# The last layer of a four-layer image network on one core: nine shifted taps from four helper arrays, and three stacked planes a chunk in their place

## The chip, the core and the metric

The kernel runs on one core of a Trainium2 chip. The metric is the device time of one execution in microseconds. The engines are TensorE (PE; PEld is its weight loading), VectorE (DVE), ScalarE (ACT), GpSimd (POOL) and SyncE (SP), which issues most transfers; 16 DMA engines carry them.

## What is computed

Input x is 8 images of 16 channels, 128 x 128, float32. Four layers follow each other, each of the form x = x + layer(groupnorm(x)). The change touches the last one alone: a 3 x 3 convolution with Kolmogorov-Arnold bases. Cut to what matters:

```python
patches = _extract_patches(x, 3, 1, 1)          # nine shifted copies, zero padded
bspl = _b_splines(patches, grid)                # eight cubic bases of each value
base_w = base_weight.sum(axis=2)
spl_w = (spline_weight * spline_scaler[..., None]).sum(axis=2)
out = jnp.einsum('bjhwn,ijn->bihw', jax.nn.silu(patches), base_w)
out = out + jnp.einsum('bjhwns,ijns->bihw', bspl, spl_w)
out = out + bias_weight[None, :, None, None]
x = x + out
```

## The kernel before

The layers run one after the other, each in blocks that end in a barrier. The first three (norm0 and layer0, layer1, layer2) stay as they are; layer2 leaves its result in the DRAM array out2, 16 channels by 8 images, each image as rows of 129 columns with padding. layer3 has two blocks.

The first block prepares. SP loads x2 (128 partitions: 8 images x 16 channels) and the eight images of out2 (L1385, each to 16 partitions). DVE adds them (L1420), copies the sum into a padded layout (L1421), takes the statistics (Norm.vector_part, L97 to L110) and normalises into Y (L1424). ACT applies silu to all of it (L1436). SP stores three arrays: x3q, the sum; g3q, the normalised input; s3q, its silu (L1388, L1391, L1394).

The second block starts with the weights (L1479) and with clearing on POOL (L1532). Its main loop walks the 134376 padded columns (all images in one line) in 66 passes of 2036 columns, plus one to finish. In a pass:

- SP loads gx, 16 channels of g3q broadcast to eight groups of 16 partitions, one group for each basis (L1487); si and si0, silu at the nine taps, each tap 16 channels from s3q (L1493, L1494); xr, the sum, in four quarters of 509 columns (L1496). It stores four quarters of the pass before the last into oq (L1501).
- ACT makes |x/h + place| (L1548), two relus (L1551, L1553) and their squares (L1556, L1558). DVE multiplies to cubes and adds them to the bases B (L1586, L1588, L1591).
- PE convolves: 8 matmuls for silu (L1608) and nine taps for the bases (L1617), each with 16 outputs padded to 32 columns of the array, one quarter in each of the four column groups.
- DVE adds bias and xr (L1579) and so gives SP leave (o_done) to load silu and xr of the pass after the next.

At the end SP copies oq to the output.

```python
for r, p in enumerate(AROUND):
    sp.dma_start(si[r * C:(r + 1) * C, k, :], s3q[:, bass.ds(g * SUP + (MARGIN + OFFS[p]), SUP)]).then_inc(si_in[k], 16)
```

The code of both blocks follows.

Of the kernel before, what the change touches and what calls it, by code (L numbers as in the profile page):

```python
# [4 lines left out]
F32 = mybir.dt.float32  # L5
# [6 lines left out]
P = 128  # L12
# [7 lines left out]
SUB = 509  # L20
# [10 lines left out]
MARGIN = 256  # L31
assert MARGIN >= max(OFFS)
# [1324 lines left out]
GRID_STEP = 2.0 / 5  # L1357

def layer3(nc, x2, out2, pair, l3w, x3q, g3q, s3q, oq, out):

    with ExitStack() as ctx:
        def sem(name):
            return ctx.enter_context(nc.semaphore(name))

        with ExitStack() as ctx1:
            def sb1(name, shape, dt=F32):
                return ctx1.enter_context(nc.sbuf_tensor(name, shape, dt))

            norm = Norm(nc, ctx1, "n3")
            X = sb1("l3_x", [P, HW])  # L1370
            Y = sb1("l3_y", [P, IMG])
            XP = sb1("l3_xp", [P, IMG])
            zero = sb1("l3_zero", [C, MARGIN + SUP])
            x_in, y_in = sem("l3_x_in"), sem("l3_y_in")
            chain = sem("l3_chain")
            x_ready, g_ready, s_ready, zeroed = sem("l3_x_ready"), sem("l3_g_ready"), sem("l3_s_ready"), sem("l3_zeroed")
            x_stored, stored = sem("l3_x_stored"), sem("l3_stored")

            with nc.Block() as block:
                @block.sync  # L1380
                def _(sp):
                    norm.sync_part(sp, pair)
                    sp.dma_start(X[:], x2).then_inc(x_in, 16)
                    for b in range(NB):
                        sp.dma_start(Y[b * C:(b + 1) * C, :], out2[:, SUP + b * IMG:SUP + (b + 1) * IMG]).then_inc(y_in, 16)  # L1385
                    sp.wait_ge(x_ready, 1)
                    for b in range(NB):
                        sp.dma_start(x3q[:, SUP + b * IMG:SUP + (b + 1) * IMG], XP[b * C:(b + 1) * C, :]).then_inc(x_stored, 16)  # L1388
                    sp.wait_ge(g_ready, 1)
                    for b in range(NB):  # L1390
                        sp.dma_start(g3q[:, b * IMG:(b + 1) * IMG], Y[b * C:(b + 1) * C, :]).then_inc(stored, 16)  # L1391
                    sp.wait_ge(s_ready, 1)
                    for b in range(NB):
                        sp.dma_start(s3q[:, MARGIN + SUP + b * IMG:MARGIN + SUP + (b + 1) * IMG], XP[b * C:(b + 1) * C, :]).then_inc(stored, 16)  # L1394
                    sp.wait_ge(zeroed, 1)

                    sp.dma_start(x3q[:, 0:SUP], zero[:, 0:SUP]).then_inc(stored, 16)
                    sp.dma_start(s3q[:, 0:MARGIN + SUP], zero[:]).then_inc(stored, 16)
                    sp.dma_start(s3q[:, MARGIN + SUP + LINE:], zero[:, 0:MARGIN]).then_inc(stored, 16)
                    sp.wait_ge(x_stored, NB * 16)  # L1400
                    sp.wait_ge(stored, (2 * NB + 3) * 16)

                @block.gpsimd
                def _(pool):
                    g = nc.gpsimd
                    g.memset(zero[:], 0.0).then_inc(zeroed, 1)
                    pool.wait_ge(x_ready, 1)

                    g.memset(Y[:, 0:PW], 0.0).then_inc(zeroed, 1)
                    g.memset(Y[:, PW:PW + H * PW].rearrange("p (h w) -> p h w", w=PW)[:, :, 0:1], 0.0).then_inc(zeroed, 1)  # L1410
                    g.memset(Y[:, PW + H * PW:], 0.0).then_inc(zeroed, 1)

                @block.vector
                def _(dve):
                    v = nc.vector
                    link = Chain(dve, chain)
                    link(v.memset(XP[:], 0.0))
                    dve.wait_ge(x_in, 16)
                    dve.wait_ge(y_in, NB * 16)
                    link(v.tensor_tensor(X[:], X[:], image_rows(Y), ALU.add))  # L1420
                    v.tensor_copy(image_rows(XP), X[:].rearrange("p (h w) -> p h w", w=W)).then_inc(x_ready, 1)  # L1421
                    norm.vector_part(dve, link, lambda k, n: X[:, k * n:(k + 1) * n], lambda e, k: None)
                    dve.wait_ge(zeroed, 4)
                    v.tensor_scalar(image_rows(Y), X[:].rearrange("p (h w) -> p h w", w=W), norm.rstd[:], norm.shift[:],  # L1424
                                    ALU.mult, ALU.add).then_inc(g_ready, 1)

                @block.tensor
                def _(pe):
                    norm.tensor_part(pe)

                @block.scalar
                def _(act):
                    norm.scalar_part(act)
                    act.wait_ge(g_ready, 1)
                    act.wait_ge(x_stored, NB * 16)
# [9 lines left out]
        wba = sb("l3_wba", [P, 2, 32])
        place = sb("l3_place", [P, 1])
        ends = sb("l3_ends", [P, 2])
        cbias = sb("l3_cbias", [P, 1])
        gx = sb("l3_gx", [P, 2, SUP])
        a = sb("l3_a", [P, SUP])  # L1450
        b = sb("l3_b", [P, SUP])
        a2 = sb("l3_a2", [P, SUP])
        b2 = sb("l3_b2", [P, SUP])
        B = sb("l3_bases", [P, BODY, SUP])
        si = sb("l3_si", [P, 2, SUP])
        si0 = sb("l3_si0", [P, 2, SUP])
        xr = sb("l3_xr", [P, 2, SUB])
# [12 lines left out]
        out_stored = sem("l3_out_stored")  # L1470
        stored = [sem("l3_o_stored0"), sem("l3_o_stored1")]
        STORE = NSUB * 16


        with nc.Block() as block:
            @block.sync
            def _(sp):
                for t, src in ((sw, l3w[0]), (scaler, l3w[1]), (bw, l3w[2]), (place, l3w[3]), (cbias, l3w[4])):
                    sp.dma_start(t[:], src).then_inc(w_in, 16)  # L1479
                sp.sem_inc(stored[0], 16)  # L1480
                sp.sem_inc(stored[1], 16)
                sp.wait_ge(cleared, 7)

                def load_bases_input(g, k, used):
                    sp.wait_ge(b_done, used)
                    src = g3q[:, bass.ds(g * SUP, SUP)].unsqueeze(0).broadcast_to([SPLINE, C, SUP])
                    sp.dma_start(gx[:, k, :], src).then_inc(gx_in[k], 16)  # L1487

                def load_silu(g, k):

                    sp.wait_ge(o_done, g + 1)
                    for r, p in enumerate(AROUND):
                        sp.dma_start(si[r * C:(r + 1) * C, k, :], s3q[:, bass.ds(g * SUP + (MARGIN + OFFS[p]), SUP)]).then_inc(si_in[k], 16)  # L1493
                    sp.dma_start(si0[0:C, k, :], s3q[:, bass.ds(g * SUP + MARGIN, SUP)]).then_inc(si_in[k], 16)  # L1494
                    for j in range(NSUB):
                        sp.dma_start(xr[32 * j:32 * j + C, k, :], x3q[:, bass.ds(g * SUP + j * SUB, SUB)]).then_inc(si_in[k], 16)  # L1496

                def store(g, k):
                    sp.wait_ge(o_done, g + 3)
                    for j in range(NSUB):  # L1500
                        sp.dma_start(oq[:, bass.ds(g * SUP + j * SUB, SUB)], O[32 * j:32 * j + C, k, :]).then_inc(stored[k], 16)  # L1501


                load_bases_input(0, 0, 1)
                for g in (0, 1):
                    load_bases_input(g + 1, (g + 1) % 2, g + 2)
                    load_silu(g, g)
# [253 lines left out]
```

## Time and profile before

| | us |
|---|---|
| median of 3 runs | 12673.22 |
| lowest and highest run | 12641.55, 12675.93 |
| span of the profiled execution | 12712.6 |
| PE busy | 9605.2 (76%) |
| DVE busy | 8869.0 (70%) |
| ACT busy | 7643.8 (60%) |
| POOL busy | 4796.5 (38%) |

The profiled execution's own time is given by its span alone, from its first instruction to its last; it is 39 us above the median. Busy time is a sum over all four layers, so it says little of the last one; views with a window do. A granted clock of 0.5 is 1.2 GHz, one of 1.0 is 2.4 GHz. DMA share is the mean busy share of the 16 DMA engines.

### The profile page before, as it was taken

How to read it: one execution, taken by the hardware profiler on the slowest of the kernel's cores; microseconds unless marked ns; L12 is line 12 of the kernel's file. 1: busy time of each engine (PE TensorE's matmuls, PEld its weight loads, DVE VectorE, ACT ScalarE, POOL GpSimd, SP SyncE). 2: the span in 40 equal slices, each digit the busy share in tenths (PEclk: the TensorE clock that was granted, in tenths of full speed). 3: DMA queues.
4: the chain of work that ended last, by engine and by line, in shares of the span. 5: the costliest groups of instructions: out<-in, count | busy, mean ns of one | idle time of the engine just before them, and what ended most of it. 6: DMA issues, size and time to landing. Idle time of an engine off the chain costs nothing. (4 is left out here: it accounts for less than half of the span.)

```text
span 12712.6 us, 210890 instructions
## 1 busy us (share of the span) xinstructions
PE 9605.2 (76%) x53759; PEld 4432.6 (35%) x53759; DVE 8869.0 (70%) x10861; ACT 7643.8 (60%) x11063; POOL 4796.5 (38%) x2382
## 2 busy tenths in 40 slices
PE   0888588868885888400999999999999999905565
PEld 0566366646663666100222222222222222202222
DVE  1877478748774777374888888888888888823343
ACT  0555255525552554232888888888888888815454
POOL 0333123212221322001666666666666666600000
PEclk9899689969996999755999999999999999957787
DMA  2000100010000000143111111111111111077787
GB/s 82 1 0 0 34 1 0 3 31 0 0 9 25 0 0 0 54 129 108 28 28 28 28 28 28 28 29 31 31 28 28 28 28 28 22 145 130 126 144 142
DMA packets 266253, 512.62 MB, mean 40 GB/s; under 512 B 46221, under 2 KB 205565, under 8 KB 260317
## 3 DMA queue, kind: packets, MB, share of 16 engines
q1 hardware_dynamic: 265314, 502.02, 18.1%
q8 instruction: 356, 5.83, 0.2%
q14 instruction: 583, 4.77, 0.1%
HBM read 368.49 MB, written 141.74 MB: 40 GB/s over the span
## 5 line engine op out<-in xcount | busy, mean ns | idle before, releaser
L1196 POOL TENSOR_TENSOR l_a<-l_a 128x1018 f32<-128x1018 f32 x1851 | 3453.2, 1883 | 1693.4 <-ACT l_a L1341 1678.5
L1311 DVE TENSOR_TENSOR l_r<-l_pps,l_a 128x509 f32<-128x509 f32 x4755 | 2988.7, 677 | 48.7 <-PE l_pps L1210 30.5
L1335 ACT ACTIVATE l_a<-l_qps 128x509 f32<-128x509 f32 x3705 | 2157.7, 597 | 822.0 <-PE l_qps L1210 568.8
L1341 ACT ACTIVATE l_a<-l_a 128x1018 f32<-128x1018 f32 x2380 | 2504.3, 1052 | 39.8 <-issue 39.8
L1210 PE MATMUL l_qps<-l_mv,l_wst 123*128 123x509 bf16 x4235 | 1645.0, 389 | 172.3 <-ACT l_a L1335 54.2
L1210 PE MATMUL l_pps<-l_mv,l_wst 123*128 123x509 bf16 x4228 | 1626.2, 385 | 63.7 <-DVE l_r L1311 60.9
L654 POOL TENSOR_TENSOR a_pr<-a_pr 128x768 f32<-128x768 f32 x384 | 898.4, 2339 | 1641.6 <-DVE a_pr L569 1626.6
L683 ACT ACTIVATE a_g<-a_fps 128x512 f32<-128x512 f32 x1152 | 680.6, 597 | 1023.7 <-PE a_fps L436 1022.3
L436 PE MATMUL a_fps<-a_hbt,a_wfc 96*128 96x512 f32 x2304 | 1238.1, 674 | 70.4 <-ACT a_g L683 70.4
L407 PEld LDWEIGHTS a_cps<-a_wfp,a_g 128*128 128x128 f32 x9216 | 1139.1, 200 | 207.7 <-issue 158.1
L1299 DVE TENSOR_SCALAR l_a<-l_qps 128x509 int32<-128x509 int32 x1058 | 724.7, 685 | 688.7 <-PE l_qps L1210 678.2
L454 POOL TENSOR_TENSOR a_pr<-a_qkv 128x768 f32<-128x768 f32 x128 | 386.5, 3037 | 2088.8 <-ACT a_qkv L696 2088.8
L407 PE MATMUL a_cps<-a_wfp,a_g 128*128 128x48 f32 (+1 forms) x9216 | 1126.5, 281 | 40.9 <-DVE a_x2c L582 40.9
L1266 PE MATMUL l_sps<-l_r,l_sums 128*32 128x509 f32 x8448 | 1132.3, 608 | 8.6 <-DVE l_r L1311 8.2
L1210 PEld LDWEIGHTS l_qps<-l_mv,l_wst 123*128 123x128 bf16 x4235 | 407.8, 96 | 2080.6 <-ACT l_a L1335 1414.9
L1305 DVE TENSOR_TENSOR l_a<-l_a 128x1018 f32<-128x1018 f32 x529 | 800.0, 1512 | 89.6 <-ACT l_a L1341 88.6
L569 DVE TENSOR_TENSOR a_pr<-a_qkv,a_at 128x768 f32<-128x768 f32 x576 | 810.1, 1459 | 2.2
L1608 PE MATMUL l_ops<-l_si,l_wba 128*32 128x509 f32 x1072 | 217.6, 954 | 612.9 <-DMA l_xr<-x3q 572.2
L436 PEld LDWEIGHTS a_fps<-a_hbt,a_wfc 96*128 96x128 f32 x2304 | 428.1, 211 | 580.6 <-ACT a_g L683 341.4
L1210 PEld LDWEIGHTS l_pps<-l_mv,l_wst 123*128 123x128 bf16 x4228 | 413.5, 98 | 506.8 <-DVE l_r L1311 365.5
L1225 PE MATMUL l_ops<-l_s,l_pick 128*32 128x509 f32 (+5 forms) x5360 | 571.4, 512 | 0.0
L1617 PE MATMUL l_ops<-l_bases,l_wsp 128*32 128x509 f32 (+8 forms) x5896 | 566.8, 538 | 0.0
(169 smaller groups left out, 11983.2 us busy)
## 6 DMA issues: line engine op xcount, KB each, us to landing
l_mv<-pw SPq DMA_DIRECT2D x1608, 79.5 KB
l_si<-s3q SPq DMA_DIRECT2D x603, 127.2 KB, 8.1
l_gx<-g3q SPq DMA_DIRECT2D x66, 1018.0 KB
pw<-pw_hi SPq DMA_DIRECT2D x165, 127.2 KB
pw<-pw_mid SPq DMA_DIRECT2D x165, 127.2 KB
pw<-pw_lo SPq DMA_DIRECT2D x165, 127.2 KB
a_tb<-g SPq DMA_DIRECT2D x16, 1031.9 KB
out<-l_o SPq DMA_DIRECT2D x268, 31.8 KB, 2.8
```

What stands on the lines that cost most here:

```text
L407: last = t_.matmul(cps[:, c % 2, j * F2 + lo:j * F2 + hi], G[:, g % 2, m, j * P:(j + 1) * P], wfp[:, m, lo:hi], start=m == 1, stop=m == 2, ...
L436: t_.matmul(fps[:, n % 2, :], wfc[:, m * P:(m + 1) * P], hBT[:, g * 4:(g + 1) * 4, :].rearrange("f w h -> f (w h)"), start=True, stop=True ...
L569: v.tensor_tensor(out, val, a, ALU.mult).then_inc(val_v, 1)
L654: g_.tensor_tensor(y, y, PR[:, 3 * d + e, :], ALU.add).then_inc(val_p, 1)
L1196: g.tensor_tensor(a, a, a, ALU.mult).then_inc(sq_p, 2)
L1210: return t.matmul(out, wst[:, k, n * P:(n + 1) * P], x[:, n // NPP, cols], start=True, stop=True)
L1266: last = t.matmul(sps[32 * pp:32 * pp + 32, 0:SUB], sums[:, 0, :], R[:, (m - NPP + 1 + pp) % R_RING, :], start=n == NPP - 1, stop=n == NPA ...
L1299: v.tensor_scalar(A[:, s % A_RING, :].bitcast(I32), qps[:, s % Q_BANKS, 0:SUB].bitcast(I32), 0x7FFFFFFF, None, ALU.bitwise_and).then_inc(a ...
L1305: v.tensor_tensor(a, a, a, ALU.mult).then_inc(sq_v, 2)
L1311: v.tensor_tensor(R[:, m % R_RING, :], pps[:, m % P_BANKS, 0:SUB], A[:, m % A_RING, :], ALU.mult).then_inc(mul_done, 1)
L1335: s_.activation(A[:, s % A_RING, :], qps[:, s % Q_BANKS, 0:SUB], ACT.Abs).then_inc(abs_a, 1)
L1341: s_.activation(a, a, ACT.Abs_reciprocal_sqrt, bias=1.0).then_inc(root_done, 2)
```

## The change

Only layer3 and its weights' layout change. Chunks are now four image rows of 130 columns (CHN = 520), 33 chunks with the padding. A chunk has two units, e = 0 and 1, each of four images side by side (2080 columns).

- Preparation: x2 and out2 come in eight pieces of 16 rows, and DVE adds and takes statistics piece by piece. The sum stays in SBUF (X). Only the normalised input is stored, into g3, chunk by chunk. The weights are loaded and summed in this block too.
- Bases: ACT makes the distance (L1543) and two squares; the two slopes now come from DVE (L1591, L1593), POOL subtracts the cubes (L1625, one operation a unit).
- Spline part: for each dx one matmul with 48 of 64 output columns, the three tap rows dy stacked on the output partitions; both units side by side in the array. ACT copies the planes to SBUF, and PE adds the three planes with shifted rows by 0/1 matrices (pick).
- Silu part: computed on ACT once a chunk (L1550) from gs, which holds the normalised input of two image rows of taps, dy = 0 in the lower 64 partitions and dy = 1 in the upper; gs is loaded by six transfers a chunk, and has one buffer.
- The result is added into X and stored from there into the output.

The diff, cut to the order on the queues and the operations of the new loop:

```diff
@@ layer3, first block @@
-                    for b in range(NB):
-                        sp.dma_start(Y[b * C:(b + 1) * C, :], out2[:, SUP + b * IMG:SUP + (b + 1) * IMG]).then_inc(y_in, 16)
...
+                    for k in range(PIECES):
+                        n = HW // PIECES
+                        sp.dma_start(X[:, k * n:(k + 1) * n], x2[:, k * n:(k + 1) * n]).then_inc(x_in[k], 16)
+                        if k >= 3:
+                            sp.wait_ge(added, k - 2)
+                        at = SUP + PW + k * ROWS * PW
+                        rows = out2[:, SUP:].rearrange("c (b n) -> b c n", b=NB)[:, :, at - SUP:at - SUP + ROWS * PW]
+                        sp.dma_start(Y[:, k % 3, :], rows).then_inc(x_in[k], 16)
...
+                        for j in range(QUAD):
+                            to = g3[lo:hi, :, :, j, :].rearrange("k e c n -> (e c) k n")
+                            src = G[32 * j:32 * j + 32, lo * CROWS:hi * CROWS, :].rearrange("p (k r) w -> p k (r w)", r=CROWS)
+                            sp.dma_start(to, src).then_inc(g_stored, 16)
@@ layer3, second block, SP @@
-                def load_silu(g, k):
-
-                    sp.wait_ge(o_done, g + 1)
-                    for r, p in enumerate(AROUND):
-                        sp.dma_start(si[r * C:(r + 1) * C, k, :], s3q[:, bass.ds(g * SUP + (MARGIN + OFFS[p]), SUP)]).then_inc(si_in[k], 16)
...
+                for n in range(NUNIT):
+                    k, e = divmod(n, PARITY)
+                    if n >= GX:
+                        sp.wait_ge(bases, n - GX + 1)
+                    src = g3[k, e].rearrange("c j n -> c (j n)").unsqueeze(0).broadcast_to([SPLINE, C, UNIT])
+                    sp.dma_start(gx[:, n % GX, :], src).then_inc(gx_in[n % GX], 16)
+                    if e == 0:
+                        if k:
+                            sp.wait_ge(silu_done, k)
+                        for h in range(HALF):
+                            rows = g3[k].rearrange("e c j n -> j (e c) n")[2 * h:2 * h + 2]
+                            sp.dma_start(gs[0:64, h, :], rows).then_inc(gs_in, 16)
+                            sp.dma_start(gs[64:P, h, 0:CHN - QW], rows[:, :, QW:]).then_inc(gs_in, 16)
+                            if k + 1 < NCK:
+                                below = g3[k + 1].rearrange("e c j n -> j (e c) n")[2 * h:2 * h + 2, :, 0:QW]
+                                sp.dma_start(gs[64:P, h, CHN - QW:], below).then_inc(gs_in, 16)
+                    elif k >= 4:
+                        store(k - 4)
@@ ACT @@
+                distance(0)
+                for n in range(NUNIT):
+                    k, e = divmod(n, PARITY)
+                    if n + 1 < NUNIT:
+                        distance(n + 1)
...
+                    s_.activation(a2[:, n % 2, :], na[:, n % 2, :], ACT.Square).then_inc(a2_done, 1)
...
+                    s_.activation(b2[:], gx[:, n % GX, :], ACT.Square, scale=2.0).then_inc(b2_done, 1)
+                    if n >= 3:
+                        for j in (0, 1) if e else (2, 3):
+                            keep((n - 3) // PARITY, j)
+                    if e == 1:
+                        silu(k)
@@ ACT, silu(k) @@
+                    pieces = (k + 1) * 6 if k + 1 < NCK else k * 6 + 4
+                    act.wait_ge(gs_in, pieces * 16)
...
+                    s_.activation(S[:, k % PSLOTS, :, :], gs[:], ACT.Silu).then_inc(silu_done, 1)
@@ DVE @@
+                    v.tensor_scalar(na[:, n % 2, :], x, 2.0, 0.0, ALU.subtract, ALU.min).then_inc(na_done, 1)
...
+                    v.tensor_scalar(x, x, 1.0, 0.0, ALU.subtract, ALU.min).then_inc(nb_done, 1)
...
+                    v.tensor_tensor(a2[:, n % 2, :], a2[:, n % 2, :], na[:, n % 2, :], ALU.mult).then_inc(a3_done, 1)
...
+                    v.tensor_tensor(gx[:, n % GX, :], b2[:], gx[:, n % GX, :], ALU.mult).then_inc(b3_done, 1)
@@ POOL @@
+                    g_.tensor_tensor(B[:, e, :, at:at + CHN], gx[:, n % GX, :].rearrange("p (j n) -> p j n", j=QUAD),
+                                     a2[:, n % 2, :].rearrange("p (j n) -> p j n", j=QUAD), ALU.subtract).then_inc(bases, 1)
@@ PE @@
+                        for dx in range(3):
+                            for e in range(PARITY):
+                                x = B[:, e, j, at:at + CHN].rearrange("p (r w) -> p r w", w=QW)[:, :, dx:dx + W]
+                                last = t.matmul(pps[64 * e:64 * e + 64, m % PBANKS, :].rearrange("p (r w) -> p r w", w=W), wsp[:, dx, :],
+                                                x, start=dx == 0, stop=dx == 2, skip_group_check=True)
...
+                    for dy in range(3):
+                        for to, n, row in pieces(k, dy):
+                            for j in range(QUAD):
+                                last = t.matmul(rows_out[32 * j:32 * j + 32, to:to + n, :], pick[:, dy, :],
+                                                planes[:, j, row:row + n, :], start=False, stop=dy == 2, skip_group_check=True)
...
+                multiply(0)
+                for k in range(NOUT):
+                    multiply(k + 1)
+                    gather(k)
```

Where the order moves, on the engines that wait. SP's queue in the main loop before, as the program lists it (the instruction, output and input tile, the size, what it waits for; "x7" is a repeat). This is a pass after the loop's unrolled part:

```order
L1487 DMA l_gx<-g3q 128x1x2036 [waits l3_b_done]
L1493 DMA l_si<-s3q 16x2036 [waits l3_o_done]
L1493 DMA l_si<-s3q 16x2036 x7
L1494 DMA l_si<-s3q 16x2036
L1496 DMA l_xr<-x3q 16x509 x4
L1501 DMA oq<-l_o 16x509 [waits l3_o_done]
L1501 DMA oq<-l_o 16x509 x3
```

And SP's queue in the changed kernel, one chunk of the steady loop, from gs(k) to the first load for gs(k+1):

```order
L1525 DMA l_gs<-g 64x1x520 [waits l3_silu_done]
L1526 DMA l_gs<-g 64x1x390
L1529 DMA l_gs<-g 64x1x130
L1525 DMA l_gs<-g 64x1x520
L1526 DMA l_gs<-g 64x1x390
L1529 DMA l_gs<-g 64x1x130
L1519 DMA l_gx<-g 128x1x2080 [waits l3_bases_ready]
L1512 DMA out_x<-l_x 128x512 [waits l3_o_done]
L1519 DMA l_gx<-g 128x1x2080 [waits l3_bases_ready]
L1525 DMA l_gs<-g 64x1x520 [waits l3_silu_done]
```

The silu input has moved behind a wait for ACT's silu of the chunk before, and the input of the chunk's second unit stands behind it.

ACT's queue in the changed kernel, from one silu to the next (l_gx<-l_gx is the distance, l_planes the copies of planes, l_s<-l_gs the silu):

```order
L1550 ACTIVATE l_s<-l_gs 128x1040 [waits l3_o_made,l3_gs_in]
L1543 ACTIVATE l_gx<-l_gx,l_place 128x2080 [waits l3_gx_in1]
L1568 ACTIVATE l_a<-l_na 128x2080 [waits l3_na_done,l3_bases_ready]
L1572 ACTIVATE l_b<-l_gx 128x2080 [waits l3_b3_done,l3_nb_done]
L1557 ACTIVATE l_planes<-l_pps 128x512 [waits l3_o_made,l3_plane_made] x2
L1543 ACTIVATE l_gx<-l_gx,l_place 128x2080 [waits l3_gx_in2]
L1568 ACTIVATE l_a<-l_na 128x2080 [waits l3_na_done,l3_bases_ready]
L1572 ACTIVATE l_b<-l_gx 128x2080 [waits l3_b3_done,l3_nb_done]
L1557 ACTIVATE l_planes<-l_pps 128x512 [waits l3_o_made,l3_plane_made] x2
L1550 ACTIVATE l_s<-l_gs 128x1040 [waits l3_o_made,l3_gs_in]
```

Silu and the copies of planes are new on ACT, the two relus have left it, and the first instruction behind a silu is a distance.

## Rows read from the trace of the kernel before

**Rows 1.** The page: DMA share in 40 slices, and the chain that ended last.
```profile
DMA  2000100010000000143111111111111111077787
...
DMA l_xr<-x3q 4%; PE l_ops L1617 2%; PE l_ops L1608 1%; SPq L1493 1%; SPq L1496 0%; DVE l_o L1579 0%; SPq L1494 0%; POOL l_bases L1532 0%; DVE l_bases L1591 0%; DVE l_a L1586 0%; DVE l_b L1588 0%; SPq L1501 0%; SPq L1487 0%; POOL l_si L1532 0%; DVEq L1578 0%
```

**Rows 2.** Windows: length, busy PE, PEld, DVE, ACT, POOL; clock, DMA share, GB/s.
```profile
11150.00:11415.00 265.00, 1.14 (x4) 1.00 (x4) 70.08 (x46) 17.03 (x4) 2.60 (x4) 0.50 0.81 163
11415.00:11430.00 15.00, 0.00 (x0) 0.00 (x0) 0.00 (x0) 0.00 (x0) 14.50 (x3) 0.50 0.27 98
11430.00:12678.00 1248.00, 768.54 (x6968) 305.95 (x6968) 498.49 (x269) 625.02 (x330) 0.54 (x5) 0.78 0.77 132
12678.00:12712.60 34.60, 0.00 (x0) 0.00 (x0) 0.68 (x1) 0.00 (x0) 0.00 (x0) 0.55 0.86 246
```

**Rows 3.** Groups by line from 11430 us on: busy, mean ns | idle before.
```profile
L1608 PE MATMUL l_ops<-l_si,l_wba 128*32 128x509 f32 x1072 | 217.6, 954 | 612.9 <-DMA l_xr<-x3q 572.2 <-DVE l_bases L1591 39.8 <-DVE l_o L1579 1.0
L1586 DVE TENSOR_TENSOR l_a<-l_a 128x2036 f32<-128x2036 f32 x66 | 150.3, 2278 | 284.2 <-ACT l_a L1556 284.2
L1548 ACT ACTIVATE l_gx<-l_gx,l_place 128x2036 f32<-128x2036 f32 x66 | 131.5, 1992 | 629.5 <-DMA l_gx<-g3q 629.4
L1556 ACT ACTIVATE l_a<-l_a 128x2036 f32<-128x2036 f32 x66 | 124.4, 1885 | 3.4 <-DVE l_bases L1591 3.4
L1579 DVE SCALAR_TENSOR_TENSOR l_o<-l_ops,l_cbias,l_xr 128x509 f32<-128x509 f32 x67 | 50.2, 749 | 455.9 <-PE l_ops L1617 455.9
```

**Rows 4.** Chain of waits in the main loop: start, length, what.
```profile
11678.22 0.76 DVE l_o L1579
11685.51 21.19 DMA l_xr<-x3q
11706.83 3.62 PE l_ops L1608 x16
11710.45 8.68 PE l_ops L1617 x50
11719.28 0.76 DVE l_o L1579
```

**Rows 5.** Windows, one transfer each: 127 partitions, x2, l_y, stores of g3q, l_gx.
```profile
140.00:160.00 20.00, 0.00 (x0) 0.00 (x0) 0.00 (x0) 0.00 (x0) 0.00 (x0) 1.00 0.07 20
11155.00:11167.00 12.00, 0.00 (x0) 0.00 (x0) 12.00 (x1) 0.00 (x0) 0.00 (x0) 0.50 0.98 426
11175.00:11235.00 60.00, 0.00 (x0) 0.00 (x0) 0.00 (x0) 0.00 (x0) 0.00 (x0) 0.50 1.00 114
11310.00:11340.00 30.00, 0.00 (x0) 0.00 (x0) 0.00 (x0) 0.00 (x0) 0.00 (x0) 0.50 0.96 251
11447.00:11456.00 9.00, 0.00 (x0) 0.00 (x0) 0.00 (x0) 7.49 (x4) 0.00 (x0) 0.50 0.52 119
```
**Rows 6.** Timeline of the preparation: start, length, what.
```profile
11150.97 4.11 SPq L1385 DMA_DIRECT2D l_y<-out  x8
11247.91 17.23 DVE L1420 TENSOR_TENSOR l_x<-l_x,l_y 128x16384 f32<-128x16384 f32 x1 [80.20 <-DMA l_y<-out]
11292.90 1.02 DVE L99 BATCH_NORM_AGGREGATE n_own<-n_stats 128x2 f32<-128x192 f32 x1
...
11297.14 8.81 DVE L1424 TENSOR_SCALAR l_y<-l_x,n_rstd,n_shift 128x16384 f32<-128x16384 f32 x1
...
11415.50 0.36 SPq L1479 DMA_DIRECT2D l_sw<-in_w_spline  x1
11430.57 1.44 SPq L1487 DMA_DIRECT2D l_gx<-g3q  x2
```

**Rows 7.** The page's groups in layer 2: POOL's product, ACT's PSUM copy and root.
```profile
L1196 POOL TENSOR_TENSOR l_a<-l_a 128x1018 f32<-128x1018 f32 x1851 | 3453.2, 1883 | 1693.4 <-ACT l_a L1341 1678.5
L1335 ACT ACTIVATE l_a<-l_qps 128x509 f32<-128x509 f32 x3705 | 2157.7, 597 | 822.0 <-PE l_qps L1210 568.8
L1341 ACT ACTIVATE l_a<-l_a 128x1018 f32<-128x1018 f32 x2380 | 2504.3, 1052 | 39.8 <-issue 39.8
```

More of the change, by code:

```diff
@@ L1357, with layer3, sb @@
 GRID_STEP = 2.0 / 5
-def layer3(nc, x2, out2, pair, l3w, x3q, g3q, s3q, oq, out):
+QW = W + 2
+CROWS = 4
+CHN = CROWS * QW
+NCK = (H + 2 + CROWS - 1) // CROWS
+NOUT = H // CROWS
+PARITY, QUAD = 2, NB // 2
+UNIT = QUAD * CHN
+GX, BSLOTS, PSLOTS, PBANKS = 3, 2, 3, 6
+HALF = 2
+assert QUAD * 32 == P and NCK == NOUT + 1
+def layer3(nc, x2, out2, pair, l3w, g3, out):
     with ExitStack() as ctx:
+        def sb(name, shape, dt=F32):
+            return ctx.enter_context(nc.sbuf_tensor(name, shape, dt))
         def sem(name):
             return ctx.enter_context(nc.semaphore(name))
+        X = sb("l3_x", [P, HW])
+        wsp = sb("l3_wsp", [P, 3, 64])
+        wba = sb("l3_wba", [P, 2, 3, QUAD, C])
+        pick = sb("l3_pick", [P, 3, 32])
+        place = sb("l3_place", [P, 1])
+        cbias = sb("l3_cbias", [P, 1])
+        mask = sb("l3_mask", [P, QUAD])
         with ExitStack() as ctx1:
@@ L1367, in sb1 @@
                 return ctx1.enter_context(nc.sbuf_tensor(name, shape, dt))
+            PIECES = 8
+            ROWS = H // PIECES
             norm = Norm(nc, ctx1, "n3")
[L1370 to L1377, printed above, removed]
+            Y = sb1("l3_y", [P, 3, ROWS * PW])
+            G = sb1("l3_g", [P, NCK * CROWS, QW])
+            sw = sb1("l3_sw", [P, 9, 9, C])
+            scaler = sb1("l3_scaler", [P, 9, 9, C])
+            bw = sb1("l3_bw", [P, 9, 9, C])
+            x_in = [sem(f"l3_x_in{k}") for k in range(PIECES)]
+            w_in = sem("l3_w_in")
+            added, chain = sem("l3_added"), sem("l3_chain")
+            zeroed, g_ready, g_stored = sem("l3_zeroed"), sem("l3_g_ready"), sem("l3_g_stored")
             with nc.Block() as block:
@@ L1389, in _ @@
[L1389 to L1397, printed above, removed]
@@ L1416, in _ @@
                     link = Chain(dve, chain)
[L1417 to L1423, printed above, removed]
@@ L1445, in layer3 @@
[L1445 to L1457, printed above, removed]
@@ L1477, in _ @@
             def _(sp):
[L1478 to L1487, printed above, removed]
@@ L1498, in store @@
[L1498 to L1507, printed above, removed]
-                with sp.Fori(1, NSUP // 2 - 1) as it:
-                    for k in range(2):
-                        g = it * 2 + k
-                        load_bases_input(g + 1, 1 - k, g + 2)
-                        load_silu(g, k)
-                        store(g - 2, k)
```

335 lines of the change are left out of this document (178 added, 157 removed).

## The prediction

> **What bounds the kernel now.** Read the page first, then windows by stage, then the chain of waits inside the last stage. The page's DMA row shows the last fifth of the span at seven or eight tenths while every compute engine is at five or less, and its chain of waits ends in loads of l_xr [rows 1]. The windows give the stages [rows 2]: 265 us of preparation of the last layer (x2 plus layer 2's output, norm, stores of three helper arrays), 15 us of clearing, 1248 us of main loop, 35 us of a final copy. Everything ahead of 11150 us is untouched by the change, so the question is 1562 us against what replaces them.
>
> The main loop makes 67 passes in 1248 us, 18.6 us each. In a pass PE needs about 12 us, the three DVE operations of 2036 columns 6.8, the five ACT operations 9.7 [rows 3]. None is full. The chain repeats one piece: last matmul, DVE's finish, thirteen loads issued by SP in about 6.5 us, 21 us until the last lands, 12 us of matmul; two passes are in flight, so 41 us of it carry two [rows 4]. DMA is the bound, at 132 GB/s with a share of 0.77 [rows 2]. Why so slow? [Rows 5] hold five kinds of transfer. Whole 128-partition rows go at 426 GB/s with all engines busy. Loads that write 16 neighbouring partitions (l_y) keep all engines busy and yet move 114. The broadcast l_gx, whose outermost dimension is 8 copies, keeps a share of 0.52 busy and moves 119. Layer 0's load of 127 partitions keeps 0.07 busy, 20 GB/s. I read two things from this: the share follows the outermost dimension (8 of 16 engines, 1 of 16), and a busy engine moves 27 GB/s in the first kind, only 14 in l_gx (119 over 8.3 engines), because engines that walk blocks of partitions get in each other's way.
>
> **The change, part by part.** The span of this profile, 12712.6 us, stands 39 us (0.3%) above the median of the runs, 12673.2; I sum against the span and carry the difference over. 0.3% is also about what a measurement of this kernel can tell from no change.
>
> *Preparation.* Now: loads 11151 to 11248, add 17.2, copy, statistics, norm, normalise 8.8, store g, silu, store s, until 11415.5; first l_gx issued at 11430.6 after the clearing [rows 6]. After: x2 and out2 come in eight pieces, add and statistics follow each piece, one array is stored. The out2 pieces have an outermost dimension of 8, like l_gx: 8.45 MB at 119 GB/s is 71 us on eight engines; x2 adds 8.4 MB at 426, 20 us; the weights, 2 MB, 5 us. So 96 us, as long as now. Then the last piece, 17.2/8 for the add and four statistics at 0.6 to 0.9 (the copy and 32 of them fill the 28 us from the add's end to 11292.9), 5 us, the norm's tail 4.2 (11292.9 to 11297.1), the first normalised piece 8.8/8 = 1.1, and 8.65 MB of stores at the 251 GB/s of today's stores, 35 us, with 5 us for landing and the barrier. Start of the new loop: 11150.5 + 146 = 11297, against 11415.5 for the old one. That saves about 119 us; the l3_x copy, silu pass and two arrays of stores are gone. Bounds on the stores, which now have rows of 2080 bytes: 20 us (426 GB/s) to 65 (132 GB/s), so 90 to 134 saved.
>
> *Main loop.* 33 chunks of two units of 2080 columns. Costs per chunk, scaled from [rows 3] and [rows 7]: ACT 2 x (1.99 + 2 x 1.89) x 2080/2036 = 11.8, four copies of planes at 0.6 = 2.4, one silu of 1040 columns 1.1 (1.05 for 1018), waits between them 0.7: 16 us. DVE 4 products of 2.33, 4 slopes of about 1.2 (0.54 ns a column as in the 8.8 us of normalising), finish 0.75: 15 us. POOL 2 subtractions at 1.85 ns a column: 7.7. PE: a round of four 32-column matmuls takes 1.81 us at granted clock 0.5 (16 records, two rounds, in 3.62 [rows 4]) and 0.9 when warm (nine rounds in 8.7, the first of them still slow); 12 rounds of two 64-column matmuls for the planes, 6 for silu, 3 for the shifted adds, 21 x 0.9 = 19 us. Transfers: two l_gx of 1.06 MB at 119 GB/s, 17.8, plus l_gs. If all of this overlapped, a chunk would take some 20 us. It does not overlap, because of the order on SP and ACT.
>
> ACT runs distance(n+1) before the squares of unit n, and silu(k) at the end of unit 2k+1. SP issues l_gx(2k), then **waits for silu(k-1)**, then issues six l_gs loads, and only then l_gx(2k+1). But distance(2k+1) is the very next thing that ACT does after silu(k-1). l_gs has one buffer, so this wait can't pass early. Every chunk thus pays, one after the other: silu(k-1) done, six l_gs, l_gx(2k+1), then ACT's 16 us up to silu(k). DVE, POOL and PE are behind ACT in that circle and cover nothing of it.
>
> The l_gs price: 532 KB in six loads whose source has an outermost dimension of 2. The row of 127 partitions and that of l_gx say that such a load runs on 2 of the 16 engines. No row shows two engines. Bounds: 27 GB/s each, 9.8 us; or 11 each (132 GB/s over the 12 busy engines of the main loop), 24 us. I take 14 each, the rate of l_gx, since here too each engine walks a block of partitions: 19 us. Behind it on the same two engines come their sixteen rows of l_gx(2k+1), 133 KB each, 4.9 to 9.5 us; I take 7. First issue 0.65, landing about 2. Gap: 0.65 + 19 + 7 + 2 = 29 us (17 to 36).
> The Trainium skill, page DMA: Bandwidth & Descriptors, section "Why a DMA increments its semaphore by 16 and not by 1", says that a DMA uses the largest number up to 16 that divides the outermost sizes of both sides: 2 here, and it speaks against this change. The page SBUF — State Buffer, section "Door 1: The DMA port swizzle", says that partitions 32 apart share a port of 27.2 GB/s; the two engines start 32 apart, and by it l_gs would take 19.6 us as an estimate.
>
> PE adds one more wait. After the second pair of planes of a chunk is copied, PE does 3 rounds of shifted adds and 6 rounds of the next planes before ACT's next copies can both run. PE has idled some 25 us by then, so two rounds go at clock 0.5, as in each pass now: 3.6 + 7 x 0.9 = 10 us, against 6 of ACT work and the copy between: 3 us exposed (0 to 8).
>
> Chunk: 29 + 16 + 3 = 48 us. Loop: 33 x 48 + 30 for the last planes, sum, finish and store (in the first chunk the gap is paid as filling) = 1614. The final copy (35 us) is gone, since finish writes straight into X and out.
> Before, from 11415.5 to the end: 1297. So +317 in the loop, -119 in the preparation: **+198**, span 12911, median **12870 us**, 1.6% slower. The loop's transfers fall from 165 MB to 96 MB, and still the time rises: the bytes saved ran in parallel, the new wait doesn't.
>
> **Rivals.**
> A, faster: l_gs is cheap. Either two engines at full rate (9.8 us, then 5 for l_gx: gap 18, chunk 37) or all 16 (532 KB at 119 GB/s 4.5 us, l_gx 8.7: gap 16, chunk 35). Loop 1185 to 1251, total 12441 to 12507; up to 12600 with small rows a little slower than 27. It wins when the chunk is under 40.5 us, that is when l_gs takes under 12. For it: a single engine alone moves 17 to 20 in the 127-partition row, even in rows of 520 bytes. Against: l_gx's 14. The change would then pay mostly by its preparation.
> B, slower yet: 64-column matmuls of the two halves don't run side by side. No row has that width; only 32-column ones, four at once, are shown. Then the planes need 12 rounds instead of 6 before ACT's copies, and the exposed wait grows from 3 to about 9: chunk 54, total 13070.
> C, in between: l_gs at 20 GB/s an engine, 13 us, gap 22, chunk 41: 12640, no measurable change.
>
> **Numbers.** Forecast 0.57 (12750 to 13000), B 0.10, C 0.07, A 0.26. Point 12870. The range must keep most of A and reach to B: 12480 to 13100. Faster by over 0.3% 0.26, within 0.07, slower 0.67.
>
> **What would show it.** In the loop ACT should idle 25 to 30 us ahead of one Abs in two, released by the l_gx load, for some 900 us in all, with a DMA share near 0.13 in the second half of that idle time (eight engines and then only two at work), and about 48 us between silus. PE's granted clock stays well under 1. The new loop starts near 11297. If the gap before the odd Abs is under 20 us, A holds. If ACT waits longest for PE's planes, B. Should ACT not idle at that Abs at all, my reading of the order is wrong, and the time would be near 11950.

## The result, and the profile after

The changed kernel takes 12784.51 us (median of 4 runs, 12773.45 to 12785.26) against 12674.58 for the kernel before beside it: a ratio of 1.0087, with a 95% interval of 1.0064 to 1.0109. It is slower by 110 us, where the forecast was 198 slower. Its page, with the same parts as [rows 1]:

```profile
span 12783.1 us, 200441 instructions
...
PEclk9899689969997998755999999999999999957777
DMA  2000100010000000043111111111111111142222
...
DMA l_gx<-g 5%; DVE l_a L1606 1%; POOL l_bases L1625 1%; DVE l_na L1591 1%; ACT l_gx L1543 0%; DVE l_gx L1609 0%; PE l_pps L1652 0%; DVE l_gx L1593 0%; PE l_ops L1681 0%; ACT l_b L1572 0%; ACT l_a L1568 0%; SPq L1529 0%; SPq L1526 0%; SPq L
```

The last slices have fallen from seven and eight tenths to two: the engines that carry transfers are now mostly idle, and yet the chain ends in a transfer, l_gx. The waits of the last 1480 us of the changed kernel (engine, line, released by: us in total, times, longest):

```profile
POOL l_bases L1625 <- DVE l_gx L1609: 1219.9, 64, 195.1
ACT l_gx L1543 <- DMA l_gx<-g: 893.7, 34, 50.1
DVE l_na L1591 <- ACT l_gx L1543: 857.4, 34, 41.5
...
ACT l_planes L1557 <- PE l_pps L1652: 140.2, 66, 10.0
```

ACT waits 34 times for l_gx, 894 us in all; 34 is one in two of 66 loads and the start, which has the longest, 50.1. All else hangs on it: DVE waits for ACT and POOL for DVE. Start and end of the parts, from the timeline of the changed kernel, which answers to [rows 6]:

```profile
11262.53 10.14 DVE L1475 TENSOR_SCALAR l_g<-l_x,n_rstd,n_shift 128x2048 f32<-128x2048 f32 x8
11263.90 32.30 SPq L1429 DMA_DIRECT2D g<-l_g  x32
11300.25 0.60 SPq L1519 DMA_DIRECT2D l_gx<-g  x1
```

And the line of silu (L1550): its count, duration, first and last start.

```profile
L1550 ACT ACTIVATE l_s<-l_gs x33: 1060/1062/1077, 11349.4 to 12749.0; 128x1040 f32<-128x1040 f32 x33
```

The loop begins at 11300.25, and 32 chunks lie between the first silu and the last: (12749.0 - 11349.4)/32 = **43.7 us a chunk**. One of them, from silu to silu:

```profile
11960.40 1.06 ACT L1550 ACTIVATE l_s<-l_gs 128x1040 f32<-128x1040 f32 x1
...
11961.49 0.51 SPq L1525 DMA_DIRECT2D l_gs<-g  x1
...
11963.92 4.62 POOL L1625 TENSOR_TENSOR l_bases<-l_gx,l_a 128x2080 f32<-128x2080 f32 x1 [5.72 <-DVE l_gx L1609]
...
11964.62 2.82 SPq L1529 DMA_DIRECT2D l_gs<-g  x1
...
11967.49 1.63 SPq L1519 DMA_DIRECT2D l_gx<-g  x1
...
11986.60 2.03 ACT L1543 ACTIVATE l_gx<-l_gx,l_place 128x2080 f32<-128x2080 f32 x1 [25.14 <-DMA l_gx<-g]
...
11993.30 4.99 PE L1681 MATMUL l_ops<-l_planes,l_pick 128*32 128x512 f32 x24 [23.13 <-ACT l_planes L1557]
...
11995.78 5.51 POOL L1625 TENSOR_TENSOR l_bases<-l_gx,l_a 128x2080 f32<-128x2080 f32 x1 [27.24 <-DVE l_gx L1609]
11996.84 5.56 DVE L1593 TENSOR_SCALAR l_gx<-l_gx 128x2080 f32<-128x2080 f32 x1
...
11998.22 10.09 PE L1652 MATMUL l_pps<-l_bases,l_wsp 128*64 128x512 f32 x46
...
12003.64 0.60 ACT L1557 ACTIVATE l_planes<-l_pps 128x512 f32<-128x512 f32 x1 [1.98 <-PE l_pps L1652]
12004.13 1.06 ACT L1550 ACTIVATE l_s<-l_gs 128x1040 f32<-128x1040 f32 x1
```

The order is the forecast one: silu, six l_gs issues, l_gx behind them, and ACT idle for 25.14 us until it lands; the other 18.6 us are ACT's circle. The transfers in that gap and just behind it, in windows of 2 us (us, busy time of PE, PEld, DVE, ACT, POOL, granted clock, DMA share, GB/s):

```profile
11964.00:11966.00 2.00, 2.00 (x12) 0.70 (x10) 0.44 (x1) 0.00 (x0) 2.00 (x1) 1.00 0.13 48
11966.00:11968.00 2.00, 2.00 (x14) 0.85 (x12) 0.00 (x0) 0.00 (x0) 2.00 (x1) 1.00 0.13 48
11970.00:11972.00 2.00, 0.17 (x2) 0.00 (x0) 0.00 (x0) 0.00 (x0) 0.00 (x0) 1.00 0.56 183
...
11980.00:11982.00 2.00, 0.00 (x0) 0.00 (x0) 0.00 (x0) 0.00 (x0) 0.00 (x0) 0.50 0.55 155
...
11984.00:11986.00 2.00, 0.00 (x0) 0.00 (x0) 0.00 (x0) 0.00 (x0) 0.00 (x0) 0.50 0.46 133
...
11988.00:11990.00 2.00, 0.00 (x0) 0.00 (x0) 1.31 (x2) 2.00 (x2) 0.00 (x0) 0.50 0.14 54
```

A share of 0.13 is two engines of sixteen, and alone they move 48 GB/s, 24 each. The first bytes of l_gs move about 2 us after the end of silu, and the two engines have the time up to about 11969 to themselves, 5.5 us: some 260 KB of the 532. The l_gx, issued at 11967.49, shows in the share only after that. From then on its eight engines are at work, and so are the store of the output and the next l_gx, l_gx(2k+2), issued 1.7 and 2.8 us behind it: the share stays near a half until the wait ends. The two engines then still owe some 270 KB of l_gs and their 266 KB of l_gx, 268 KB each, and have moved them when the l_gx has landed, 17.6 us later: 15 GB/s each, worked out from the bytes. When that l_gx has landed, two engines are left with the next one, and the last window shows them at 54 GB/s with a share of 0.14, some 24 each again.

**Where the time went.** The first three layers, which the change leaves alone, do not take the same time in every execution: in the profiled executions of the table below the last layer began between 11083.8 and 11159.9. The kernel before, timed beside each group of them, had medians from 12660 to 12702, so a difference of a few tens of us between medians says little. So kernels are compared below by their medians, and by the last layer of the profile alone, from its first load of x2 or of out2 to the end. Before, that was 12712.6 - 11150.5 = 1562.1 us; after, 12783.1 - 11149.2 = 1633.9: +72.

### The profile page after: what moved, and what is told of

Read it like the earlier page. It is cut to its first block and busy times, and to the rows that moved or that the text cites. A ratio compares the mean times of both kernels' runs of the same rounds, so it can differ in the third digit from the quotient of the medians.

```text
span 12783.1 us, 200441 instructions
## 1 busy us (share of the span) xinstructions
PE 9480.8 (74%) x50455; PEld 4341.6 (34%) x50455; DVE 8979.9 (70%) x10918; ACT 7480.8 (59%) x11095; POOL 5115.3 (40%) x2443
## 5 line engine op out<-in xcount | busy, mean ns | idle before, releaser
L1625 POOL TENSOR_TENSOR l_bases<-l_gx,l_a 128x2080 f32<-128x2080 f32 x66 | 334.8, 5073 | 1269.3 <-DVE l_gx L1609 1219.9
L1681 PE MATMUL l_ops<-l_planes,l_pick 128*32 128x512 f32 (+3 forms) x928 | 147.6, 802 | 727.3 <-ACT l_planes L1557 727.3
L1591 DVE TENSOR_SCALAR l_na<-l_gx 128x2080 f32<-128x2080 f32 x66 | 81.9, 1241 | 857.4 <-ACT l_gx L1543 857.4
L1543 ACT ACTIVATE l_gx<-l_gx,l_place 128x2080 f32<-128x2080 f32 x66 | 133.7, 2025 | 893.7 <-DMA l_gx<-g 893.7
```

## The experiments

Two theories stood against each other. **Theory:** the loop waits for one chain, silu(k-1), six l_gs on two engines, l_gx(2k+1); both the order and the two engines make it. **Rival:** the bound is elsewhere (l_gx on its eight engines alone, or POOL, DVE and PE behind the loads), and the l_gs loads only hide it. Each edit was made to the changed kernel if nothing else is said.

| kernel | median us | ratio to before (95%) | last layer us | chunk us |
|---|---|---|---|---|
| changed | 12784.51 | 1.0087 (1.0064 to 1.0109) | 1633.9 | 43.7 |
| e1, l_gx first | 12420.06 | 0.9779 (0.9736 to 0.9823) | 1259.3 | 32.0 |
| e2, l_gs on 16 engines | 12545.9 | 0.9879 (0.9834 to 0.9923) | 1380.2 | 36.1 |
| e3, l_gx on 16 engines | 12655.91 | 0.9964 (0.9931 to 0.9997) | 1520.0 | 40.2 |
| e4, all three | 12116.99 | 0.9542 (0.9506 to 0.9579) | 955.9 | 23.3 |
| e5b, no l_gs | 12185.01 | 0.9604 (0.9518 to 0.9690) | 1058.6 | 26.0 |
| e9, subtraction on DVE | 12775.01 | 1.0069 (1.0040 to 1.0098) | 1646.1 | 44.0 |
| e8, e4 and e9 | 12012.99 | 0.9483 (0.9447 to 0.9519) | 888.3 | 20.9 |
| e7, kernel before, l_gx on 16 | 12391.16 | 0.9778 (0.9733 to 0.9824) | 1239.4 | |

A chunk is worked out as above, from the first and last start of silu.

**e1: both l_gx of a chunk ahead of the wait.** One place in SP's program:

```diff
-for n in range(NUNIT): wait for bases; load l_gx(n)
-    if e == 0: wait for silu(k-1); load l_gs(k)
+for n in range(NUNIT):
+    if e == 0: load_gx(n); load_gx(n + 1)
+               wait for silu(k-1); load l_gs(k)
```

> SP issues both l_gx loads of a chunk ahead of its wait for silu(k-1); nothing else changes, l_gs keeps its six loads on few engines. Order theory (the odd unit's load waits behind silu(k-1) and six l_gs loads): ACT's idle time of 25 us before every second Abs goes; what is left is what two DMA engines carry in a chunk, l_gs 14 us and two l_gx 9 us each, about 32 us against 44, so 12400 to 12450 us. Rival (the load of l_gs on two engines is the bound whatever the order): the time of l_gs and l_gx on the two engines already fills the chunk, so within 0.3% of 12784. Rival (PE's planes hold ACT): also no change beyond 2 us a chunk.

12420.06 us, as the theory says. Nothing but the order changed, and 364 us went. What is left of the gap, in its timeline:

```profile
11800.01 2.03 ACT L1548 ACTIVATE l_gx<-l_gx,l_place 128x2080 f32<-128x2080 f32 x1 [16.98 <-DMA l_gx<-g]
...
11806.55 1.06 ACT L1555 ACTIVATE l_s<-l_gs 128x1040 f32<-128x1040 f32 x1
11807.51 2.02 ACT L1548 ACTIVATE l_gx<-l_gx,l_place 128x2080 f32<-128x2080 f32 x1
...
11815.15 10.86 SPq L1519 DMA_DIRECT2D l_gx<-g  x2
...
11832.42 2.03 ACT L1548 ACTIVATE l_gx<-l_gx,l_place 128x2080 f32<-128x2080 f32 x1 [18.26 <-DMA l_gx<-g]
```

The Abs right after silu no longer waits. The wait has moved to the even unit and is shorter, 17 to 18 us: the next l_gx follows the l_gs in the queue of the same engines.

**e2: l_gs in twelve loads of 32 partitions.** The source row j of the four, taken alone, has an outermost dimension of 32:

```diff
-rows = g3[k].rearrange("e c j n -> j (e c) n")[2 * h:2 * h + 2]
-sp.dma_start(gs[0:64, h, :], rows)
+rows = g3[k].rearrange("e c j n -> j (e c) n")[j]
+sp.dma_start(gs[lo:lo + 32, h, :], rows)
```

> Order on SP as in the changed kernel; each l_gs load is cut into two of 32 partitions, with the 32 as the outermost dimension, 12 loads a chunk instead of 6. Two-engine theory: l_gs now runs on all 16 engines and takes 4 us instead of 14, but SP needs 6 us to issue twelve; the gap falls from 25 to 16 to 18 us, chunk 35 to 37, 12480 to 12550 us. Rival (l_gs is limited by its row size, not by its engines): gap unchanged or 3 us longer by the issues, 12780 to 12880.

12545.9 us, inside what the theory gave for it. The same bytes, in twice as many loads. Its DMA issues between 11360 and 12700 us (count, KB each, median us to landing):

```profile
l_gs<-g SPq DMA_DIRECT2D x124, 65.0 KB, 2.0
l_gs<-g SPq DMA_DIRECT2D x124, 48.8 KB, 1.9
l_gs<-g SPq DMA_DIRECT2D x120, 16.2 KB, 1.7
```

Each lands about 2 us after its issue, so SP's issuing, twelve in 5.5 us, is what they cost now:

```profile
11812.44 1.06 ACT L1552 ACTIVATE l_s<-l_gs 128x1040 f32<-128x1040 f32 x1
...
11813.53 0.31 SPq L1527 DMA_DIRECT2D l_gs<-g  x1
...
11818.99 0.60 SPq L1519 DMA_DIRECT2D l_gx<-g  x1
...
11830.93 2.03 ACT L1545 ACTIVATE l_gx<-l_gx,l_place 128x2080 f32<-128x2080 f32 x1 [17.43 <-DMA l_gx<-g]
```

**e3: l_gx on sixteen engines.** The basis partitions are ordered (channel, copy) instead of (copy, channel), in the load and in the weights, so that the outermost dimension is 16:

```diff
-src = g3[k, e].rearrange("c j n -> c (j n)").unsqueeze(0).broadcast_to([SPLINE, C, UNIT])
+src = g3[k, e].rearrange("c j n -> c (j n)").unsqueeze(1).broadcast_to([C, SPLINE, UNIT])
```

> The bases' partition order is turned from (copy, channel) to (channel, copy), so the broadcast source of l_gx has an outermost dimension of 16 instead of 8; weights are laid out to match. Engine-count theory: l_gx runs on 16 engines, at least 1.5 times as fast (9 us to 4 to 6); the gap falls from 25 to about 20 us because l_gx comes last in it, chunk 39, 12600 to 12660 us. Rival (l_gx is limited where it lands, not by its engines): same 9 us, within 0.3% of 12784.

12655.91 us: 129 us less, near the top of the expected range. The two engines of l_gs now owe half as much l_gx, but the six l_gs stand ahead as before, and the chunk is still 40.2 us. Of the three edits this one alone gives least.

**e4: all three.**

> The three edits together. Theory: no transfer is waited for any more; the chunk is bounded by DVE (about 19 us a chunk with its stalls beside POOL) and PE (19 us), chunk 21 to 25, 12010 to 12150 us, faster than both kernels by 4 to 5%. Rival (a second circle over PE's planes and ACT's copies takes over, 4 us of wait a chunk are seen already): chunk 27 to 30, 12220 to 12320.

12116.99 us, inside the range. The three save 668 us together, where one by one they save 364, 239 and 129, 732 in sum: they cut the same gap, so they do not quite add. One part of the expectation failed: l_gx is still waited for, now ahead of every Abs, by 3.6 to 4.8 us in the chunks around 11725, and 333.5 us in all:

```profile
ACT l_gx L1550 <- DMA l_gx<-g: 333.5, 66, 45.6
```

**e5: the l_gs loads left out** after the first chunk, so that silu is taken of chunk 0's rows 33 times and the output is not the layer's.

```diff
-if k:
-    sp.wait_ge(silu_done, k)
-load l_gs(k)
+if not k:
+    load l_gs(0)
```

> The six silu loads of every chunk but the first are left out: silu is taken of chunk 0's rows 33 times, all else stays. Theory (the gap of 25 us ahead of one Abs in two is made by these loads, which run on two of the sixteen DMA engines and stand ahead of the second l_gx): a chunk of 43.7 us falls to the circle of the three l_gx slots, some 24 to 26 us, as in the kernel with all three edits (23.3), a little above it since l_gx still runs on eight engines; 32 x 18 to 19.5 us off 12784: 12160 to 12210 us. Rival (the loads only hide a bound of the computation, POOL's subtraction and the DVE operations beside it being slower than before): the chunk stays above 30 us, 12350 us or more.

One execution took 12227.9 us; the profiled one ran with PE's granted clock at 0.27 and took 33169 us, so nothing is read from it. It was run again:

> The kernel of e5_no_gs once more: the profiled execution there took 33169 us with a TensorE clock of 0.27 in the records, and its only other execution 12228 us. As there: the silu loads of every chunk but the first are left out. Theory (the two-engine loads ahead of the second l_gx make the gap): a chunk of 24 to 26 us, 12160 to 12230 us, and no gap of 25 us ahead of an Abs in the trace. Rival (a bound of the computation behind them): chunks above 30 us, 12350 us or more.

12185.01 us and 26.0 us a chunk, the theory's numbers. So l_gs cost 17.7 of 43.7 us, with all that went with it: its 532 KB a chunk, its issues and SP's wait for silu, which the edit takes out together. The computation was no bound above 26 us. Its timeline has waits of five or six us for l_gx, ahead of every Abs, and none of 25:

```profile
11807.37 2.03 ACT L1542 ACTIVATE l_gx<-l_gx,l_place 128x2080 f32<-128x2080 f32 x1 [5.33 <-DMA l_gx<-g]
...
11820.38 2.03 ACT L1542 ACTIVATE l_gx<-l_gx,l_place 128x2080 f32<-128x2080 f32 x1 [6.36 <-DMA l_gx<-g]
```

e4 beats it by 68 us (103 by the last layer alone) while it loads everything: l_gs is hidden there, and l_gx arrives sooner.

**e6: a second buffer for the silu input** and nothing else, so that its loads need not wait for the silu of the chunk before. It was expected to take 12370 to 12530 us, or to change nothing. It gave no time: with the second buffer the planes no longer fit into SBUF (24576 bytes a partition wanted, 23872 left). What the wait alone costs, with l_gs kept ahead of l_gx, is therefore not measured.

**e7: the kernel before, with the l_gx order of e3.** If [rows 5] were read rightly, the kernel before was itself waiting for eight engines.

> The kernel before, with the basis partitions ordered (channel, copy) so that the outermost dimension of the l_gx load is 16 instead of 8. Theory (its last loop waits for eight of the sixteen engines, which the trace shows full while the mean share is 0.76): l_gx spreads over all sixteen, the loop shortens from 1297 us towards 0.76/0.98 x 1297 = 1006 us, where the engines are evenly full; 12684 - 150 to 290 = 12395 to 12535 us. Rival (the sixteen engines share one bound on what 128 partitions take in, so that the spread changes nothing): within 30 us of 12684.

12391.16 us, 2.2% faster than the kernel before and 393 us faster than the changed one. Windows of 1280 us of the loop before, and of 500 us in e7 (columns as above):

```profile
11420.00:12700.00 1280.00, 768.54 (x6968) 305.95 (x6968) 499.18 (x269) 625.02 (x330) 10.54 (x5) 0.78 0.76 133
```

```profile
11500.00:12000.00 500.00, 391.12 (x3847) 161.44 (x3839) 272.89 (x147) 350.71 (x185) 0.00 (x0) 0.90 0.98 182
```

All sixteen engines are now full, at 182 GB/s instead of 133. The rival, that 128 partitions take in no more than before, has fallen. It also gives both designs with their l_gx on sixteen engines: e4 against e7, 12117 against 12391. That is not the worth of the stacked planes alone. By the last layer e4 is 283.5 us shorter, and 131 of them lie ahead of the first l_gx, in preparation and clearing (150 us against 281).

**e9: the subtraction on DVE instead of POOL.** The profile's chain through the chunk above runs over POOL's subtraction, begun at 11963.92, to l_gx, issued at 11967.49. POOL takes 5.07 us on average and one slope on DVE takes 5.56 beside it, where the same operation alone takes 1.24.

```diff
-pool: wait for a3, b3, plane_made; g_.tensor_tensor(B[...], gx[...], a2[...], ALU.subtract).then_inc(bases, 1)
+dve:  wait for a3, b3, plane_made; v.tensor_tensor(B[...], gx[...], a2[...], ALU.subtract).then_inc(bases, 1)
```

> The changed kernel with one edit, the subtraction on DVE instead of POOL. Theory (the gap is a gap of transfers, and POOL's subtraction stands on the chain only between it and the next load into the same slot: 5.07 us on POOL beside 3.3 us slopes, against 2.3 and 1.24): 2 to 4 us of 43.7 in a chunk, 12784 - 65 to 130 = 12650 to 12720 us. Rival (the subtraction is hidden behind the gap, as the wait of the loads is for the silu of the chunk before, which follows the Abs and not the subtraction): within 35 us of 12784.

The rival is right. 12775.01 us is the changed kernel's time within the intervals, and a chunk stays at 44.0 us. The timeline shows why:

```profile
11961.72 2.03 ACT L1543 ACTIVATE l_gx<-l_gx,l_place 128x2080 f32<-128x2080 f32 x1 [25.49 <-DMA l_gx<-g]
...
11970.86 2.33 DVE L1615 TENSOR_TENSOR l_bases<-l_gx,l_a 128x2080 f32<-128x2080 f32 x1
...
11980.19 2.32 DVE L1615 TENSOR_TENSOR l_bases<-l_gx,l_a 128x2080 f32<-128x2080 f32 x1
...
11984.49 1.34 SPq L1529 DMA_DIRECT2D l_gs<-g  x1
11985.87 1.65 SPq L1519 DMA_DIRECT2D l_gx<-g  x1
```

The load of the odd unit, l_gx(2k+1), waits for the bases of unit 2k-2, whose slot it takes. Here that subtraction is done at 11973.19, and l_gx still goes out at 11985.87, behind the last l_gs issue. In the changed kernel it is this one:

```profile
11952.67 5.53 POOL L1625 TENSOR_TENSOR l_bases<-l_gx,l_a 128x2080 f32<-128x2080 f32 x1 [28.52 <-DVE l_gx L1609]
```

It ended at 11958.20, 9.3 us before the l_gx. The subtraction that the chain names runs from 11963.92 for 4.62 us, to 11968.54, and was still running when l_gx was issued; the chain cuts it off at that moment. It cannot have released this load, only l_gx(2k+2), at 11970.29.

**e8: the same edit on e4**, where the gap is gone.

> The kernel with all three edits (12117), and the subtraction that makes the bases moved from POOL to DVE. Theory (a chunk there, 23.3 us, is two thirds of the circle of one l_gx slot, some 35 us from the issue of its load to the end of the subtraction; POOL's subtraction takes 4.6 us where DVE takes 2.3, and while it runs the first DVE slope takes 3.4 us on average instead of 1.24): the circle falls by some 4 us, and DVE is busy 2 x (2 x 1.24 + 3 x 2.32) + 0.75 = 19.6 us in a chunk, which then bounds it: 20.5 to 22 us a chunk, 12117 - 32 x (1.3 to 2.8) = 12030 to 12075 us. Rival (the two engines do not slow each other, the long slope is only a wait that the profile counts as work): DVE gets 4.6 us more in a chunk, and the time stays or rises, 12100 to 12180 us.

12012.99 us, 5.2% below the kernel before and the fastest here. It lies 17 us below the expected range in the median, while the chunk, 20.9 us, lies inside it. The first slope (L1598) in e4 and then in e8, shortest, median and longest in ns:

```profile
L1598 DVE TENSOR_SCALAR l_na<-l_gx x66: 1244/3434/3839, 11307.1 to 12053.7; 128x2080 f32<-128x2080 f32 x66
```

```profile
L1598 DVE TENSOR_SCALAR l_na<-l_gx x66: 1230/1243/1246, 11293.8 to 11967.8; 128x2080 f32<-128x2080 f32 x66
```

Same operation, same data, 3.43 us beside a POOL subtraction and 1.24 without: the two engines do hold each other up, and here it counts. By the last layer alone the edit saves 67.6 us. The medians differ by 104; in the two profiles e8's last layer begins 21.8 us earlier, after layers that the edit leaves alone, and the rest of the difference is not explained by any row.

## Why the prediction came out as it did

**What bounds the kernel: right.** The engines at work follow the outermost dimension (e2, e3, e7), and l_gx on eight engines was the bound before (e7). The second reading of [rows 5], 14 GB/s for an engine of l_gx, held beside other engines. Its reason, that engines which walk blocks of partitions get in each other's way, was not tested, but two such engines alone move 24 each.

**Preparation: right.** The loop was to begin at 11297 and begins at 11300.25: the first piece is normalised at 11262.5, where the sum gave 11256, and the issues of the stores of g took 32.3 us of the 35 allowed. Some 115 us of 119 were saved.

**The order on SP and ACT: right.** This was the step on which the sign hung. The gap stands ahead of one Abs in two (893.7 us in all, the start with them, 900 forecast), released by l_gx, and reordering alone (e1) takes the chunk from 43.7 to 32.0.

**The l_gs price: too high, and the term that missed.** The gap was put at 29 us and is 25.1. "I take 14 each, the rate of l_gx" nearly holds for a load beside l_gx: the two engines move 15 GB/s each in the last 17.6 us. It does not hold for the 5.5 us before, in which l_gs is alone and they move 24 each, near the upper bound of 27. The two rates belong to one chain, and the forecast used the low one for all of l_gs. Worked out from these rates, l_gs takes 5.5 + 9 = 14.5 us where the sum had 19, and the two engines' share of l_gx 8.7 where it had 7; the first 2 us, in which no byte moves, complete the 25.1. By the issues, the gap is 6.0 us from the end of silu to the issue of l_gx and 19.1 to its landing. The Trainium skill's page DMA: Bandwidth & Descriptors, section "Why a DMA increments its semaphore by 16 and not by 1", gives 2 engines here, and the share of 0.13 agrees. The forecast's estimate from its page SBUF — State Buffer, section "Door 1: The DMA port swizzle", that two engines starting 32 partitions apart have the 27.2 GB/s of one port between them, does not hold: they moved 48. The section says which partitions share a port; that both engines are at the same port at the same moment was the forecast's own step, and no row shows where each of them stood.

**The sign in the DMA share: missed.** A share near 0.13 was to stand in the second half of the idle time, with eight engines and then only two at work. It stands at the beginning, before l_gx; the second half has 0.46 to 0.55. The forecast had left out that SP issues the next chunk's first l_gx only 2.8 us behind the one waited for: the engines that are done with that one go on with the next, beside the two that are late. This is where the 15 GB/s were measured, and no run has the two without it.

**ACT's circle and PE's wait: right in sum.** 16 + 3 = 19 forecast, 18.6 measured. ACT's exposed wait for PE is 140.2 us over the loop, 4.2 a chunk against 3. The 46 matmul records of 64 columns in the chunk above take 10.09 us. A matmul is two records, a round of the forecast two matmuls, and so a round takes 10.09 x 48/46/12 = 0.88 us, 0.9 forecast. Were the two of a pair run one after the other at 0.9 each, a round would take twice that; rival B has fallen.

**DVE and POOL: sized too low, and it cost nothing.** Slopes of "about 1.2" take up to 5.6 beside POOL, and POOL's subtraction 5.07 instead of 3.85. e9 shows that the gap hid it, e8 that it costs 2.4 us a chunk once the gap is gone.

**The sum.** 32 x (48 - 43.74) = 136 us are more than the miss in the last layer, 126: 198 forecast and 72 measured. The first chunk's filling (49.1 us against 48) and the end (34.1 against 30) give 5 back, and the preparation, 151 us from the first load against 146.5, the other 5.

**The base.** The forecast carried the 39 us by which the profile of before stood above its median over to the new kernel. The changed kernel's profile stood 1 us below its own. By the medians the change is therefore +110 and not +72. This brought the forecast of the median to within 86 us, where its sum was 126 off, and was luck. The first three layers scatter by tens of us between executions, and a shift of one profile against its median is no property of the kernel that could be carried over.

**Rivals A and C.** A needed a chunk under 40.5 us and missed it by 3.2: nearly its full rate was there, 24 of 27, but only until l_gx ran beside. C, with 20 GB/s, a gap of 22 and a chunk of 41, was nearer to the chunk (2.7 us under it, the forecast 4.3 over); by the median the forecast was nearer, 12870 against C's 12640. Between the two stood only the size of one term, and the three theories agreed on its place.

## What to carry to other kernels

Read the issuing queue as a program of its own: a load that must wait for a buffer holds up every load behind it, and the cheapest edit here, two lines in another order, was worth 364 us. For each load, look at the outermost dimension of both sides, since the bytes tell nothing of how many engines carry them; cutting or turning a load so that it is 16 or 32 took the kernel before down by 2.2% and the changed one, with the order, by 5.2%. And price a transfer by what runs beside it, once for the stretch in which it is alone and once for the rest.

## What had not been expected

- Two engines, partitions 32 apart at the start, each moved 24 GB/s as long as only l_gs was under way, 15 with two l_gx and a store beside them, and 24 again with the last of an l_gx alone. The kind of load that they carry does not explain the difference; what runs beside them may. Which of the neighbours it would be is not settled: no run took only the l_gx or only the store away.
- DVE and POOL lock each other out. A slope of 2080 columns takes 1.24 us alone, but 5.56 when POOL's subtraction is running: in the chunk above POOL runs from 11995.78 to 12001.29, and the slope that began at 11996.84 ends at 12002.40, 1.11 us after POOL, as if it had begun only then. POOL's subtraction, begun 0.2 us into the slope before, takes 5.51 us there instead of the 4.62 of the other one. The Trainium skill, page SBUF — State Buffer, section "SBUF: two separate sides", says that some DVE operations and GpSimd's share a pair of ports as an exclusive lock, held for the whole instruction; the trace agrees with its 1.11 us, and so does e8, where the slope is back at 1.24. The forecast had given both engines their own times side by side.
- SP's issue of a load on two engines stalls when several are under way: 0.5 us for the first three, up to 2.82 for the sixth, against 0.31 to 0.43 for each of the twelve in e2. The six took 6.0 us to issue, longer than the twelve with 5.5.
- PE's granted clock is 1.00 while PE works, up to 11970, and 0.50 in the idle windows from 11980 on; over 500 us of the loop it was 0.73 in the changed kernel and 0.97 in e8:

```profile
11500.00:12000.00 500.00, 228.25 (x1286) 79.54 (x1288) 218.11 (x105) 170.32 (x129) 115.39 (x23) 0.73 0.25 66
```

```profile
11500.00:12000.00 500.00, 453.42 (x2720) 163.76 (x2718) 442.67 (x255) 327.83 (x257) 0.00 (x0) 0.97 0.54 132
```

With the gap closed the matmuls have nearly the full clock as well. What bounds e8 now was not tried: DVE is busy for 443 of 500 us and PE for 453, and ACT still waits for l_gx, 214 us in all from 11300 us on:

```profile
ACT l_gx L1550 <- DMA l_gx<-g: 214.1, 45, 7.8
```
